# Attention quads with the mask added by VectorE and the maximum subtracted by GpSimd, every second one

## What is computed

```
q = layernorm(x);  k = v = ctx
s = q k^T / 4, entries above the diagonal -inf         # per sequence and head, 128 x 128
p = exp(s - rowmax(s)) ; o = (p / rowsum(p)) v
x = x + tanh(g) * o
```

## Time and profile before

| | |
|---|---|
| median of 3 runs | 875.26 us |
| profiled execution | 873.47 us |
| its span in the profile | 871.7 us |
| PE busy | 854.5 us (98%) |
| DVE busy | 583.4 us (67%) |
| ACT busy | 522.5 us (60%) |
| POOL busy | 133.4 us (15%) |
| granted TensorE clock | 0.999 |

### The profile page before, as it was taken

How to read it: one execution, slowest core, us unless ns; L and a number is a source line. 1 busy time by engine, 2 the same in 40 slices (tenths; PEclk the granted TensorE clock), 3 DMA queues, 4 the chain that set the end, 5 groups by cost and what they waited for, 6 DMA issues and landing times.

```text
span 871.7 us, 13779 instructions
## 1 busy us (share of the span) xinstructions
PE 854.5 (98%) x4683; PEld 705.3 (81%) x4700; DVE 583.4 (67%) x1225; ACT 522.5 (60%) x900; POOL 133.4 (15%) x125
## 2 busy tenths in 40 slices
PE   7999999999999999999999999999999999999998
PEld 7999887888788888877777788887888888888886
DVE  4998754565735665599989776569655566666664
ACT  3334434343554444456786867777777877777774
POOL 7997100000111210013223300000000000000000
PEclk9999999999999999999999999999999999999999
DMA  8230232324366833166684054444444344444433
GB/s 282 114 121 32 83 105 91 112 92 143 108 207 207 245 110 96 30 170 188 196 231 138 9 189 123 146 144 136 136 135 125 119 145 146 144 146 146 145 121 108
DMA packets 77348, 119.04 MB, mean 137 GB/s; under 512 B 9888, under 2 KB 36800, under 8 KB 76896
## 3 DMA queue, kind: packets, MB, share of 16 engines
q1 hardware_dynamic: 77072, 118.08, 43.9%
q10 hardware_dynamic: 208, 0.09, 0.0%
HBM read 96.81 MB, written 12.94 MB: 126 GB/s over the span
## 4 chain that ended last, share of the span: by engine, by line
PE 84%; DVE 7%; DMA 2%; POOL 2%; issue 2%; ACT 1%; SPq 1%; DVEq 0%; ACTq 0%; POOLq 0%
PE bank L714 39%; PE bank L750 29%; PE bank L1616 3%; PE bank L1627 2%; PE bank L1607 1%; PE bank L1238 1%; PE bank L1239 1%; DVE max L1813 1%; PE bank L1257 1%; PE bank L1636 1%; DVE y L1819 1%; DMA x_mixed<-in_x 1%; PE bank L383 1%; PE bank L365 1%; POOL weighted L1112 1%
## 5 line engine op out<-in xcount | busy, mean ns | idle before, releaser
L496 ACT ACTIVATE y_hi<-y 128x512 fp32r<-128x512 f32 x200 | 124.1, 621 | 79.9 <-DVE y L596 79.1
L610 DVE TENSOR_TENSOR y<-y,gate_rows 128x512 f32<-128x512 f32 x124 | 85.7, 691 | 117.0 <-ACT y L485 115.1
L750 PE MATMUL bank<-y_hi,w_hi 128*128 128x512 f32 x400 | 156.9, 392 | 1.5 <-DVE y_lo L330 1.5
L750 PE MATMUL bank<-y_hi,w_lo 128*128 128x512 f32 x400 | 155.8, 389 | 0.0
L750 PE MATMUL bank<-y_lo,w_hi 128*128 128x512 f32 x400 | 155.7, 389 | 0.0
L330 DVE TENSOR_TENSOR y_lo<-y,y_hi 128x512 fp32r<-128x512 f32 x196 | 134.3, 686 | 29.9 <-ACT y_hi L496 29.6
L479 ACT ACTIVATE activated<-bank 128x512 f32<-128x512 f32 x136 | 81.2, 597 | 77.2 <-PE bank L714 70.1
L714 PE MATMUL bank<-x_hi_first,w_hi 128*128 128x512 f32 x264 | 105.1, 398 | 0.7 <-DVE w_lo L325 0.7
L714 PE MATMUL bank<-x_hi_last,w_hi 128*128 128x512 f32 x264 | 103.9, 394 | 0.0
L714 PE MATMUL bank<-x_hi_first,w_lo 128*128 128x512 f32 x264 | 103.0, 390 | 0.0
L714 PE MATMUL bank<-x_hi_last,w_lo 128*128 128x512 f32 x264 | 102.9, 390 | 0.0
(11 more groups left out here) (160 smaller groups left out, 1312.4 us busy)
## 6 DMA issues: line engine op xcount, KB each, us to landing
gate_rows<-gates SPq DMA_DIRECT2D x156, 256.0 KB, 3.7
w_raw<-in_wu SPq DMA_DIRECT2D x68, 256.0 KB, 2.6
w_raw<-in_wu SPq DMA_DIRECT2D x32, 384.0 KB, 3.3
k_parts<-xn_split SPq DMA_DIRECT2D x64, 128.0 KB, 2.0
k_blocks<-k_parts SPq DMA_DIRECT2D x64, 128.0 KB, 2.9
q_split_t<-xn_split SPq DMA_DIRECT2D x64, 128.0 KB, 2.7
v_slot<-in_v_rows SPq DMA_DIRECT2D x16, 256.0 KB, 3.7
ctx_windows<-in_ctx_win SPq DMA_DIRECT2D x3, 1024.0 KB, 14.0
```

What stands on the lines that cost most here:

```text
L496: act.activation(mem.yhi[:, K % S, :], mem.y[:, K % S, :], ACT.Copy).then_inc(s_yh, 1)
L610: dve.tensor_tensor(mem.y[:, K % S, :], mem.y[:, K % S, :], gate, ALU.mult).then_inc(s_yd, 1)
L750: last = pe.matmul(acc(s)[:, c, :], w_[:, Nu % S, wc], y_[:, K % S, :], start=(n == 0 and m == 0), stop=(n == U - 1 and m == 2), skip_grou ...
```

## The change

Quads with odd n from 3 to 55 (27 of 64) go another way:

- `scores(n)` has no mask matmul; each of its two halves starts its own sum.
- VectorE adds the bf16 mask to the bank and writes the slot in SBUF (`masked`, which frees the bank), then takes the maxima from the slot (`masked_maxima`).
- GpSimd subtracts the maximum from the slot in place (`shifted_by_pool`), and `turned(n)` waits for that.

TensorE's list computes scores one quad further ahead, and once-a-block work is moved: `inverse` and `scaled` from t = 3 to the next block's t = 0, `residual` to t = 1 behind the subtraction, `moments` to t = 2, `query_normed` and `query_hi` to t = 0, `query_lo` to t = 3, `query_turned` from t = 0 to the t = 3 before it, `query_copy` to t = 0. The splitting of the next stage's rows on VectorE goes to quads 51, 52, 59 and 60 from 50, 51, 58 and 59.

```diff
+            def by_pool(n):
+                return n % 2 == 1 and SR <= n < NQ - 8
...
             def scores(pe, n):
...
-                pe.matmul(s_bank(n), identb[:], causal[:].rearrange("p h k -> p (h k)"), start=True, stop=False)
+                if not by_pool(n):
+                    pe.matmul(s_bank(n), identb[:], causal[:].rearrange("p h k -> p (h k)"), start=True, stop=False)
...
             def turned(pe, n):
-                pe.wait_ge(s_d, n + 1)
+                if by_pool(n):
+                    pe.wait_ge(s_ps, by_pool_to(n))
+                else:
+                    pe.wait_ge(s_d, n + 1)
...
             def c_gpsimd(pool):
+                def shifted_by_pool(n):
+                    pool.wait_ge(s_m, n + 1)
+                    pool.tensor_tensor(Ds[:, n % DR], Ds[:, n % DR],
+                                       nmax[:, n % DR, :].unsqueeze(2).broadcast_to((P, 4, P)), ALU.subtract).then_inc(s_ps, 1)
                 for n in range(NQ):
-                    if t == 2 and b + 3 < NB:
+                    if by_pool(n):
+                        shifted_by_pool(n)
+                    if t == 1 and b > 1:
+                        residual(pool, b - 2)
+                    if t == 3 and b + 3 < NB:
                         query_lo(pool, b + 3)
-                    if t == 3 and b > 0:
+                    if n == NQ - 1:
                         residual(pool, b - 1)
...
             def c_tensor(pe):
+                def scores_at(n):
+                    if n == 0:
+                        return (2, 3)
+                    if n == 3:
+                        return (6, 7)
+                    return tuple(m for m in (n + 3 if n < 3 else n + 4,) if m < NQ)
...
-                    if n + SR < NQ:
-                        scores(pe, n + SR)
+                    for m in scores_at(n):
+                        scores(pe, m)
...
-                    if n == 52:
+                    if n == 51:
                         pe.wait_ge(f1.s_l, 2)
...
-                    if t == 0 and b > 0 and b + 2 < NB:
-                        query_turned(pe, b + 2)
+                    if t == 3 and b + 3 < NB:
+                        query_turned(pe, b + 3)
...
             def c_vector(dve):
                 def maxima(n):
                     dve.wait_ge(s_s, n + 1)
+                    if n >= DR and by_pool(n - DR):
+                        dve.wait_ge(s_ps, by_pool_to(n - DR))
...
+                def masked(n):
+                    if n == SR:
+                        dve.wait_ge(s_cc, 32)
+                    dve.wait_ge(s_s, n + 1)
+                    if n >= DR:
+                        dve.wait_ge(s_tt, n - DR + 1)
+                    dve.tensor_tensor(Ds[:, n % DR], s_bank(n).rearrange("p (h k) -> p h k", k=P), causal[:], ALU.add).then_inc(s_d, 1)
+
+                def masked_maxima(n):
+                    dve.wait_ge(s_d, n + 1)
+                    dve.tensor_reduce(nmax[:, n % DR, :], Ds[:, n % DR], AX_X, ALU.max).then_inc(s_m, 1)
```

More of the change, by code:

```diff
@@ L1572, in attention @@
             s_gf = sem("c_gate_column")
+            s_ps = sem("c_shifted_by_pool")
             s_m = sem("c_max")
@@ L1585, in s_bank, with by_pool_to @@
                 return bk(n % SR)
+            def by_pool(n):
+                return n % 2 == 1 and SR <= n < NQ - 8
+            def by_pool_to(n):
+                return sum(1 for m in range(n + 1) if by_pool(m))
             o_bank, row_bank = bk(6), bk(7)
@@ L1607, in scores @@
                     last = pe.matmul(s_bank(n)[:, a * 2 * P:(a + 1) * 2 * P], Q1[:, b % 2, a, t, :], blocks[:, :, a, :],
-                                     start=False, stop=(a == 1))
+                                     start=by_pool(n), stop=(by_pool(n) or a == 1))
                 last.then_inc(s_s, 1)
             def turned(pe, n):
-                pe.wait_ge(s_d, n + 1)
+                if by_pool(n):
+                    pe.wait_ge(s_ps, by_pool_to(n))
+                else:
+                    pe.wait_ge(s_d, n + 1)
                 if n >= 2:
@@ L1729, in c_tensor @@
                         f0.out_turned(pe, 1, 0, 0, x_bank)
-                    if n == 0:
-                        scores(pe, 2)
-                    if n + SR < NQ:
-                        scores(pe, n + SR)
+                    for m in scores_at(n):
+                        scores(pe, m)
                     if n == 0:
@@ L1744, in c_tensor @@
                         f0.out_turned(pe, 1, 1, 1, row_bank)
-                    if n == 4:
+                    if n == 3:
                         pe.wait_ge(f0.s_xa, 7)
-                    if n == 52:
+                    if n == 51:
                         pe.wait_ge(f1.s_l, 2)
@@ L1787, in c_scalar @@
                     b, t = n // 4, n % 4
-                    if t == 1 and b > 0 and b + 2 < NB:
+                    if t == 0 and b > 0 and b + 2 < NB:
                         query_copy(act, b + 2)
@@ L1804, in c_scalar @@
                         f1.w_hi(act, n - NQ + 8)
-                    if t == 1 and b + 3 < NB:
+                    if t == 0 and b + 3 < NB:
                         query_normed(act, b + 3)
-                    if t == 2 and b + 3 < NB:
                         query_hi(act, b + 3)
@@ L1825, in c_vector @@
                     b, t = n // 4, n % 4
-                    if n + 1 < NQ:
+                    if by_pool(n + 1):
+                        masked(n + 1)
+                    elif n + 1 < NQ:
                         maxima(n + 1)
-                    if t == 3 and b > 0:
+                    if t == 0 and b > 1:
+                        inverse(dve, b - 2)
+                    if n == NQ - 1:
                         inverse(dve, b - 1)
-                    if t == 1 and b > 1:
+                    if t == 2 and b > 1:
                         moments(dve, b - 2)
-                    if n + 1 < NQ:
+                    if by_pool(n + 1):
+                        masked_maxima(n + 1)
+                    elif n + 1 < NQ:
                         shifted(n + 1)
@@ L1841, in c_vector @@
                         negated(dve, "c", 1)
-                    if n in (50, 58):
+                    if n in (51, 59):
                         f1.x_lo(dve, b // 2 - 6, 0, row_bank)
-                    if n in (51, 59):
+                    if n in (52, 60):
                         f1.x_lo(dve, b // 2 - 6, 1, x_bank)
-                    if n in (55, 63):
-                        f1.logits_copy(dve, b // 2 - 6, x_bank)
-                    if t == 3 and b > 0:
+                    if n in (56, 63):
+                        f1.logits_copy(dve, 0 if n == 56 else 1, x_bank)
+                    if t == 0 and b > 1:
+                        scaled(dve, b - 2)
+                    if n == NQ - 1:
                         scaled(dve, b - 1)
```

## The result

| | before | after |
|---|---|---|
| median of 7 runs | 875.01 us (874.03 to 876.27) | 879.76 us (878.42 to 885.26) |
| profiled execution, its span | 873.47, 871.7 | 878.42, 876.6 |
| ratio of the runs | | 1.0064, 95% interval 1.0047 to 1.0082 |

The change makes the kernel slower, by about 5 us. The forecast of 874.7 (871.3 to 878.2) is wrong in sign and in range. The profiled executions differ by 4.95 us.

What follows compares the result with a forecast made beforehand. TensorE was taken as the bound from quad 15 on, VectorE before. Masks -4.2, fill +1.3 - 0.65, old stall -0.78, queries +0.84 + 1.0 + 1.6, row waits +0.3 sum to -0.6 us: 874.7, range 871.3 to 878.2.

Steps and rivals of the forecast that it cites:

- Waits at quads 50 and 51: TensorE waits for row splits VectorE does one iteration later: 0 to 1.2 us, mostly under the stall before; 0.3 taken.
- GpSimd's load: In a steady attention block, two subtractions, residual and lower part take 4.1 of 5.9 us, so GpSimd keeps up.
- the rivals: Four alternatives: queries no bound (20%), half of it (15%), query issues held in most blocks (17%), GpSimd slower (5%).
- the one on the slower side: Query issues held in most blocks, 0.93 us for each; five held give 878.3 us; chance 17%.
- the forecast of "same": Whole kernel within 0.2%, 1.75 us, of the time before; chance 43%, with its own range of 873.2 to 876.6.
- Mask matmuls: TensorE, odd quads 19 to 55: 19 masks removed at 0.22 us each save 4.2 us.
- Fill: At the regime change turned(15) comes 1.3 us later; TensorE one quad of scores further ahead gives -0.65.
- VectorE, GpSimd: VectorE stays at 5.82 us a block at no cost; GpSimd's subtraction takes 1.29 us and it keeps up.
- its latency is hidden by the three slots: GpSimd's subtraction on the path to turned(n) is hidden with 0.4 us to spare; otherwise 16 us over 27 quads.
- Queries: First scores of blocks wait for query transfers: 0.84 us from the 6.02 us loop over seven blocks, 1.0 from held issues.
- a wait for ScalarE: Crowding of ScalarE at t = 0 can delay values by 0 to 0.2 us a block; overlaps the query stall, taken as 0.
- The 1.6 for quad 52: Quad 52's queries, behind a weight load, stall TensorE 1.1 to 2.1 us, 1.6 taken, replacing the 0.78 stall of before.

Runs made afterwards that it cites:

- e2: Changed kernel with GpSimd's four w_lo of the next stage one quad later, so residual(12) stands ahead of them; 875.36 us, 1.0011 of the kernel before.
- e10: Changed kernel with residual(12) alone done by VectorE right before moments(12), w_lo left in place; 876.63 us, 1.0008 of the kernel before.
- e4: Changed kernel with all moves but nothing handed to GpSimd: every mask on TensorE, every subtraction on VectorE; 879.95 us, 1.0072 of the kernel before.
- e8: Changed kernel with all moves, nothing handed to GpSimd, and its w_lo one quad later; 876.26 us, 1.0024 of the kernel before.
- e1: Changed kernel with the values' load issued behind the queries on SyncE's queue instead of ahead; 879.98 us, 1.0056 of the kernel before.

## Why the prediction was wrong

*The moved steps, the step that failed.* The sum had 0.3 us for all waits near the end ("Waits at quads 50 and 51"), and the moves of `residual` and `moments` had no term. It read GpSimd's load (4.1 of 5.9 us) and not its order: nothing in it says which instruction of GpSimd's list `residual` is moved behind, and that is `w_lo(0)` in the last blocks. Found: 4.2 us (32.25 against 28.08 in e2). VectorE stands still for 2.92 us, which gives TensorE 1.8 and 1.2 us of idleness, 2.75 us of the block's time, and then the lower clock for some 4 us, 1.55 more. The order is shown by e2 and e10; the clock's part did not come in e4, where the same step cost 2.7 us. None of the rivals had it; the one on the slower side was about query issues. With it mended (e2) the kernel stands at 1.0011, and the forecast of "same" would have held, in part by luck: the masks gave 1.4 us less than forecast and the queries cost 1.2 less.

*Mask matmuls: right mechanism, wrong size.* 0.22 us was read in one place of the list, behind `query_turned`, and used for all 19. It holds for quads whose scores come at t = 3; at t = 1 it is 0.07. With nine of the one and ten of the other, 10 x 0.22 + 9 x 0.07 = 2.8 us for 4.2.

*Fill.* Forecast were +1.3 and -0.65, the second since TensorE's scores are one quad further ahead. By iteration 14 +0.97 is found. The second term was about right in size, but it comes at the end: the block from 58 to 62 has one set of scores fewer (0.45) and a wait for VectorE less (0.23), and takes 5.58 us in e2, e4 and e8 for 6.27 before, -0.69. Together +0.3.

*VectorE, GpSimd.* VectorE's block is 5.81 us, from one `masked` to the same one four quads later in the kernel after:

```profile
405.83 0.68 DVE L1854 TENSOR_TENSOR y<-bank,causal 128x512 f32<-128x512 f32 x1
...
411.64 0.68 DVE L1854 TENSOR_TENSOR y<-bank,causal 128x512 f32<-128x512 f32 x1
```

as forecast (5.82). GpSimd was busy 3.74 and 3.57 us in the two later blocks shown above, for 4.1 forecast. The new operations, by group over the whole span (count, busy us, mean ns, idle before):

```profile
L1854 DVE TENSOR_TENSOR y<-bank,causal 128x512 f32<-128x512 f32 x27 | 18.3, 678 | 0.0
...
L1858 DVE TENSOR_REDUCE max<-y 128x4 f32<-128x512 f32 x27 | 17.7, 654 | 0.1
...
L1720 POOL TENSOR_TENSOR y<-y,max 128x512 f32<-128x512 f32 x27 | 28.1, 1041 | 77.6 <-DVE max L1858 77.6
```

The subtraction is 1.04 us, not 1.29, so 1.5 times VectorE's 0.69 and not about twice. The reading that its latency is hidden by the three slots held: in all of the attention the weight loads of the transposes waited 2.9 us for it, in six places, all before iteration 14, where VectorE is the bound; the prediction's estimate for a subtraction on the path of every quad was 16.

```profile
DVE stats L1690 <- POOL X L1686: 4.2, 3, 2.9
...
PEld bank L1627 <- POOL y L1720: 2.9, 6, 0.8
```

(Waits of the kernel after from 366 to 488 us: total, times, longest.)

*Queries.* The stalls came as described, at the first scores of a block, and four of eight blocks have one, of 0.4 to 0.7 us. Forecast were 0.84 + 1.0 in the seven blocks; found is 2.56 above 8 x 6.07 from 14 to 46, in which is a wait for ScalarE of about 0.4 at 450.27, in the longest block (6.90), that was put at nothing. The 1.6 for quad 52 did not come: its scores, in iteration 48, waited for no transfer, and the 0.78 of before went. So the queries cost 2.2 us where 3.4 were forecast.

*Waits at quads 50 and 51.* TensorE's weight loads in the kernel after:

```profile
457.99 0.42 PEld L1647 LDWEIGHTS bank<-ident,o_t 128*128 128x128 f32 x4 [0.76 <-DVE x_lo_first L375]
...
460.13 0.39 PEld L1508 LDWEIGHTS bank<-ident_r,xn_split 128*128 128x128 f32 x4 [0.73 <-DVE x_lo_first L375]
```

Less the 0.20 that both have anyway, about 1.1 us for 0.3: the stall of quad 52 that was to hide them was not there.

Together, from the -0.6 of the forecast: +4.2 (order on GpSimd), +1.4 (masks), -0.4 (fill and the quad ahead), +0.8 (row waits), +0.4 (ScalarE), -1.2 (queries) and 0.5 ahead of the attention make +5.1, where the profiled executions differ by 4.95. That it closes so well is more than the single terms bear, since the stretches scatter by up to 1.6 us.

## What to carry to other kernels

When a step is moved in the list of an in-order engine, write down what now stands ahead of it there, for every iteration in which the list differs, the first and last blocks above all, and what those instructions wait for; load (busy over period) says nothing about it. Lists that run at different distances ahead of each other must not be crossed: a step that a leading engine (here VectorE, two quads ahead) needs must not stand behind one that waits for a trailing engine (ScalarE). And an operation's price on TensorE is read at each place where it stands, since taking it out can leave a gap in its place.

## What the runs showed of the hardware

- After 1.8 and 1.2 us of idleness (TensorE busy 1.49 of 4.00 us, 472 to 476) its clock was granted at 0.55 and 0.60 for the next 4 us of full work, and at 1.00 after it: the stall cost 2.75 us and the clock 1.55 more. In e1 it fell behind the same two waits too, in e4, on the same chip as e1, it stayed at 1.00. So such a stall can bring the lower level and need not; what decides it no run here shows. By the Trainium skill (TensorE: Matmul & The Clock Gate, Part 1: What's actually happening) a gate passes only a part of TensorE's clock pulses after it has been little busy, which leaves 1.2 GHz. The traces of after and e1 agree with that, and the one of e4 shows that these waits are not always enough.
- GpSimd subtracted 512 elements a partition in 1.04 us where one operand is a repeated column (27 times), and took 1.27 to 1.34 with two full ones (subtractions at L325 and L330, an addition at L1112).
- A DMA issue of keys or queries took 0.60 us at the median, and in blocks of the attention now and then 1.1 to 2.2 (the longest in e4), without a wait that the profile shows.
- Executions of one kernel differed by up to 11 us (878.42 to 885.26 in 7 of the one after, 875.00 to 886.10 in 12 of e8), part of it outside the attention (e10 entered it 4.5 us later than after did): the stretches between marks tell more than single times, and even they scatter by up to 1.6 us.
